# A two-layer perceiver on one core: SP's last stores and loads in another order, two projections and their norms in one block by halves

## The reference, cut to what matters

```python
x = x + xattn0(ctx, layernorm(x), mask)   # 16 heads of 16, masked
x = x + attn0(layernorm(x))               # causal, spectrally scaled weights
x = x + experts(layernorm(x))             # top 3 of 12, two mixtures
x = x + xattn1(layernorm(x), ctx, ctx)    # 16 heads of 64, with a norm of its own
x = x + attn1(layernorm(x))               # covariance scores
x = x + ffn(layernorm(x))                 # quantised, gated
# layernorm(x) = (x - mean) / sqrt(var + 1e-5), over the 256 features
# each attention ends with  out @ Wo ; attn0's Wo is scaled by sigma
```

## Time and profile before

| | us |
|---|---|
| three runs, median (lowest, highest) | 1699.28 (1698.58, 1701.09) |
| the profiled execution, its own time | 1701.46 |
| its span, first to last instruction | 1699.7 |
| PE, DVE, ACT, POOL busy | 1549.9, 1102.9, 890.6, 694.0 |
| mean granted TensorE clock | 0.954 of full |

### The profile page before, as it was taken

How to read it: one execution, slowest core, us unless ns; L and a number is a source line. 1 busy time by engine, 2 the same in 40 slices (tenths; PEclk the granted TensorE clock), 3 DMA queues, 4 the chain that set the end, 5 groups by cost and what they waited for, 6 DMA issues and landing times. The chain is left out here.

```text
span 1699.7 us, 42063 instructions
## 1 busy us (share of the span) xinstructions
PE 1549.9 (91%) x15983; PEld 878.0 (52%) x15983; DVE 1102.9 (65%) x1783; ACT 890.6 (52%) x1205; POOL 694.0 (41%) x539
## 2 busy tenths in 40 slices
PE   7999999999499999999777969999999999996784
PEld 3454554554134343433453426777777777773442
DVE  4656656665499999997327756666666666604546
ACT  5555555554178888888251015555555555541535
POOL 5340000000011111111152209999999999960710
PEclk9999999999689999999898979999999999997897
DMA  7987979877522222221400057555555546212000
GB/s 240 224 239 213 224 232 227 224 213 178 175 79 67 66 67 66 67 67 34 159 2 1 0 143 225 156 159 141 139 156 161 150 121 161 77 36 94 2 1 13
DMA packets 178502, 212.23 MB, mean 125 GB/s; under 512 B 57380, under 2 KB 151856, under 8 KB 173768
## 3 DMA queue, kind: packets, MB, share of 16 engines
q1 hardware_dynamic: 177800, 210.44, 44.9%
q10 hardware_dynamic: 576, 0.00, 0.0%
HBM read 122.78 MB, written 87.57 MB: 124 GB/s over the span
## 5 line engine op out<-in xcount | busy, mean ns | idle before, releaser
L1227 POOL TENSOR_TENSOR x_r<-x_p 128x1024 f16<-128x1024 f32 x256 | 479.3, 1895 | 24.1 <-ACT x_p L1203 17.3
L1242 DVE TENSOR_REDUCE x_mx<-a_all 128x2 f32<-128x1024 f32 x249 | 304.9, 1225 | 147.1 <-PE a_all L1126 147.1
L1203 ACT ACTIVATE x_p<-s_all 128x1024 f32<-128x1024 f32 x256 | 248.4, 1022 | 223.5 <-PE s_all L1109 223.5
L801 ACT ACTIVATE x_p<-s_all 128x1024 f32<-128x1024 f32 x256 | 261.7, 1025 | 60.4 <-PE s_all L708 55.0
L849 DVE TENSOR_REDUCE x_mx<-a_all 128x1 f32<-128x512 f32 x352 | 232.0, 683 | 32.3 <-PE o_all L717 23.2
L1109 PE MATMUL s_all<-x_q,x_k 64*128 64x256 f16 x3072 | 210.2, 270 | 0.0
L1144 PEld LDWEIGHTS o_all<-x_v,x_p 128*128 128x128 bf16 x2048 | 178.7, 97 | 40.1 <-issue 40.1
L1144 PE MATMUL o_all<-x_v,x_p 128*128 128x129 f16 x2048 | 197.3, 221 | 0.9 <-POOL x_r L1227 0.9
L1145 PE MATMUL o_all<-x_v,x_r 128*128 128x65 f16 x2048 | 192.5, 193 | 0.0
L1109 PEld LDWEIGHTS s_all<-x_q,x_k 64*128 64x128 f16 x3072 | 149.5, 94 | 62.2 <-issue 0.8
L1145 PEld LDWEIGHTS o_all<-x_v,x_r 128*128 128x128 f16 x2048 | 180.7, 98 | 0.0
(11 more groups left out here) (367 smaller groups left out, 2759.8 us busy)
## 6 DMA issues: line engine op xcount, KB each, us to landing
values<-vst SPq DMA_DIRECT2D x16, 2064.0 KB, 11.2
x_v<-values SPq DMA_DIRECT2D x32, 1032.0 KB, 5.4
keys<-kst SPq DMA_DIRECT2D x32, 1024.0 KB, 6.9
x_k<-keys SPq DMA_DIRECT2D x128, 256.0 KB, 5.1
wf<-keys SPq DMA_DIRECT2D x192, 64.0 KB, 2.2
values<-vst SPq DMA_DIRECT2D x16, 528.0 KB, 11.6
x_v<-values SPq DMA_DIRECT2D x32, 264.0 KB, 2.6
cf<-in_ctxT SPq DMA_DIRECT2D x16, 512.0 KB, 9.9
```

The costliest lines, as they stand in the source:

```text
L801: act.activation(prob[g % NP][:], chip.s_ps[g % 2][:].rearrange("p (c q) -> p c q", q=SQ), ACT.Exp, scale=hd ** -0.5).then_inc(p_ready, 1)
L1203: act.activation(prob[g % NP][:], chip.s_ps[g % 2][:].rearrange("p (c q) -> p c q", q=SQ), ACT.Exp, scale=hd ** -0.5).then_inc(p_ready, 1)
L1227: pool.tensor_tensor(rest[g % NP][:], prob[g % NP][:], hi, ALU.subtract).then_inc(rest_done, 1)
L1242: dve.tensor_reduce(mx[a[1] % 2][:, n // 4, 2 * (n % 4):2 * (n % 4) + 2], chunk_banks(u, g)[:, :].rearrange("p (h c) -> p h c", h=2), AX.X ...
```

## The change

It has two parts. In SP's program the wait for the query stores and the query loads of w = 0, 1 go behind the last chunk's small stores and the key loads of w = 2, 3; those of w = 2, 3 go into the next block, behind the values of w = 0; the wait for the loads at the end of the block goes. And at two places `project_and_norm` stands for `rows_project` and `layer_norm`: one block, in which transposes, copies, statistics, power, normalising and the second transposes and copies work on two row tiles at a time. ScalarE now copies both halves of the normalised rows.

```diff
--- before
+++ after
@@ project_context, SP's step @@
                             sp.wait_ge(small_stored, 48)
                             for w in range(2, 4):
                                 cross.load_keys(sp, 0, w)
+                            sp.wait_ge(queries.out, 32)
+                            for w in range(2):
+                                cross.load_queries(sp, 0, w)
...
@@ project_context, SP's end @@
                 step(PAIRS - 1, 0, True)
                 queries.stores(sp)
-                sp.wait_ge(queries.out, 32)
-                for w in range(4):
-                    cross.load_queries(sp, 0, w)
                 step(PAIRS - 1, 1, True, final=True)
                 sp.wait_ge(stage_free[0], PAIRS * OUTS * 16 + 16)
                 for w in range(4):
-                    sp.wait_ge(cross.loaded[w], 16 * 12)
                     sp.wait_ge(cross.rows_in[w], 16 * 6)
...
@@ cross_attention_small, SP's start @@
                 sp.dma_start(fold_sb[:], fold).then_inc(fold_in, 16)
-                for w in range(W):
+                buffers.load_values(sp, 0, 0)
+                for w in range(2, W):
+                    buffers.load_queries(sp, 0, w)
+                for w in range(1, W):
                     buffers.load_values(sp, 0, w)
...
+class HalfNorm:
...
+    def stats_of(self, dve, t, src):
+        dve.bn_stats(self.st[:, t, :], src).then_inc(self.stats, 1)
+
+    def variance(self, dve, h):
+        dve.wait_ge(self.stats, 2 * h + 2)
+        for t in (2 * h, 2 * h + 1):
+            dve.bn_aggr(self.mv[:, t, :], self.st[:, t, :]).then_inc(self.spread, 1)
+        dve.wait_ge(self.spread, 2 * h + 2)
+        hs = slice(2 * h, 2 * h + 2)
+        dve.tensor_scalar(self.ve[:, hs], self.mv[:, hs, 1], 1e-5, None, ALU.add).then_inc(self.var, 1)
+
+    def power(self, pool, h):
+        hs = slice(2 * h, 2 * h + 2)
+        pool.wait_ge(self.var, h + 1)
+        pool.tensor_tensor(self.rs[:, hs], self.ve[:, hs], self.chip.half[:, hs], ALU.pow).then_inc(self.rstd, 1)
+
+    def apply(self, dve, t, out, src):
+        dve.wait_ge(self.rstd, t // 2 + 1)
+        dve.tensor_scalar(out, src, self.mv[:, t, 0:1], self.rs[:, t:t + 1], ALU.subtract, ALU.mult).then_inc(self.normed, 1)
+
+    def turn(self, pe, h):
+        pe.wait_ge(self.normed, 2 * h + 2)
+        for k in range(KT):
+            for t in range(2):
+                last = pe.transpose(self.banks[h][:, (2 * k + t) * P:(2 * k + t + 1) * P],
+                                    self.chip.xn[:, 2 * h + t, k * P:(k + 1) * P], self.chip.ident[:])
+        last.then_inc(self.turned, 1)
+
+    def copy(self, act, h):
+        act.wait_ge(self.turned, h + 1)
+        act.activation(self.chip.xnT[:, :, h * 2 * P:(h + 1) * 2 * P], self.banks[h].rearrange("p (k t) -> p k t", k=KT),
+                       ACT.Copy).then_inc(self.copied, 1)
+
+def project_and_norm(chip, tag, src, weight, finish):
...
+            def _(pool):
+                for h in range(2):
+                    norm.power(pool, h)
...
+            def _(pe):
+                for h in range(2):
+                    for k in range(KT):
+                        for t in range(2):
+                            last = pe.transpose(chip.s_banks[h][:, (2 * k + t) * P:(2 * k + t + 1) * P],
+                                                src[:, 2 * h + t, k * P:(k + 1) * P], chip.ident[:])
+                    last.then_inc(tr, 1)
+                pe.wait_ge(weight.loaded, 16)
+                for t in range(NT):
+                    pe.wait_ge(tr_out, t // 2 + 1)
+                    for k in range(KT):
+                        last = pe.matmul(chip.banks[t][:, 0:D], srcT[:, k, t * P:(t + 1) * P], w[:, k, :],
+                                         start=(k == 0), stop=(k == KT - 1))
+                    last.then_inc(ready, 1)
+                for h in range(2):
+                    norm.turn(pe, h)
...
+            def _(act):
+                for h in range(2):
+                    act.wait_ge(tr, h + 1)
+                    act.activation(srcT[:, :, h * 2 * P:(h + 1) * 2 * P], chip.s_banks[h].rearrange("p (k t) -> p k t", k=KT),
+                                   ACT.Copy).then_inc(tr_out, 1)
+                for h in range(2):
+                    norm.copy(act, h)
...
+            def _(dve):
+                for h in range(2):
+                    for t in (2 * h, 2 * h + 1):
+                        dve.wait_ge(ready, t + 1)
+                        finish(dve, t, done)
+                        dve.wait_ge(done, t + 1)
+                        norm.stats_of(dve, t, chip.x[:, t, :])
+                    norm.variance(dve, h)
+                for t in range(NT):
+                    norm.apply(dve, t, chip.xn[:, t, :], chip.x[:, t, :])
...
@@ perceiver @@
-                rows_project(chip, "o0", att, D, wo, add_to_x(chip))
-            layer_norm(chip, "ln1")
+                project_and_norm(chip, "o0", att, wo, add_to_x(chip))
...
-                rows_project(chip, "o1", att, D, wo, finish)
-                layer_norm(chip, "ln2")
+                project_and_norm(chip, "o1", att, wo, finish)
```

More of the change, by code:

```diff
@@ L1271, in _, with __init__ @@
                 output((PAIRS - 1, W - 1))
+class HalfNorm:
+    def __init__(self, chip, tag, scope, banks):
+        self.chip, self.banks = chip, banks
+        self.st = chip.sb(f"{tag}_st", [P, NT, 6], F32, scope)
+        self.mv = chip.sb(f"{tag}_mv", [P, NT, 2], F32, scope)
+        self.ve = chip.sb(f"{tag}_ve", [P, NT], F32, scope)
+        self.rs = chip.sb(f"{tag}_rs", [P, NT], F32, scope)
+        (self.stats, self.spread, self.var, self.rstd, self.normed, self.turned, self.copied) = (
+            chip.sem(f"{tag}_{n}") for n in ("stats", "aggr", "var", "rstd", "xn", "tr", "trout"))
+    def stats_of(self, dve, t, src):
[25 more added lines that the diff above has]
+                       ACT.Copy).then_inc(self.copied, 1)
@@ new lines, in project_and_norm @@
+def project_and_norm(chip, tag, src, weight, finish):
+    nc = chip.nc
+    with ExitStack() as scope:
+        w = weight.w
+        srcT = chip.sb(f"{tag}_srcT", [P, KT, TOK], F32, scope)
+        norm = HalfNorm(chip, f"{tag}_ln", scope, chip.s_banks[2:4])
+        tr, tr_out, ready, done = (chip.sem(f"{tag}_{n}") for n in ("tr", "trout", "rdy", "done"))
+        with nc.Block() as block:
+            @block.gpsimd
+            def _(pool):
+                for h in range(2):
+                    norm.power(pool, h)
+            @block.tensor
+            def _(pe):
[14 more added lines that the diff above has]
+                    norm.turn(pe, h)
+            @block.scalar
+            def _(act):
[5 more added lines that the diff above has]
+                    norm.copy(act, h)
+            @block.vector
+            def _(dve):
[8 more added lines that the diff above has]
+                    norm.apply(dve, t, chip.xn[:, t, :], chip.x[:, t, :])
```

## The result

| us | before | after |
|---|---|---|
| median (lowest to highest) | 1699.83 (1698.58 to 1701.09), 4 runs | 1685.08 (1679.71 to 1686.66), 4 runs |
| the profiled execution | 1701.46 | 1686.49 |
| its span | 1699.7 | 1684.8 |
| mean granted TensorE clock | 0.954 | 0.956 |

The kernel is faster by 14.75 us: ratio 0.9898, with a 95% interval of 0.9881 to 0.9914. The prediction, 1681.6 in a range of 1677.5 to 1687.5, had the sign and the size, and is 3.5 us too low at the median.

The account below looks back on a forecast made before the run. The prediction took SP's program order, and projection, barrier and norm in sequence at two places, as the limits. Gains 8.2 + 8.4 + 1.1 = 17.7 us took the median from 1699.28 to 1681.6, range 1677.5 to 1687.5.

Parts of the forecast that it names:

- SP's order: End of the cross attention's preparation: issuing small stores earlier starts the small attention 8.2 us sooner, bounds 12.2 and 3.2.
- Rival (a): Before the small attention: the small stores land late, SP's reordering gives only 3.2 us, total 1686.6; chance 0.12.
- Rival (e): Before the small attention: another wait near 452 replaces SP's, reordering gains nothing, total 1689.8; chance 0.03.
- The cover for w = 2: In the small attention: w = 2 queries land 5 us before TensorE wants them; beyond that each us late costs one.
- The halved projections: Behind cross attention and self-attention: projection and norm by two tiles gain 8.4 us together, bounds 2.2 and 8.9.
- The clock: At self-attention's start: shorter TensorE idle may hold its clock; a quarter of 4.2 us, 1.1 us, was counted.
- Rival (b): At self-attention's and the experts' start: TensorE's clock holds at both, 3.1 us more gain, total 1678.5; chance 0.17.
- Rival (c): In both norms: GpSimd's powers and VectorE exclude each other, four powers of 0.71 cost 2.8 us, total 1684.4; chance 0.10.

Follow-up runs that it names:

- part 2: The changed kernel with the query loads of w = 2 and 3 moved behind all values and the four weights; one run took 1691.17 us.
- part 3: The changed kernel, but the first pair's normalising waits for both powers, so it runs beside neither; one run took 1688.47 us.
- the kernel with products: Changed kernel, w = 0, 1 queries before small-store wait, causal-mask wait delayed to first scores, six unread products per norm gap; 1679.92 us, again 1681.65.
- Norms alone: Only the two projections with their norms by halves, SP's program as in the kernel before; 1691.78 us, ratio 0.9942.
- part 5: GpSimd's split waits for only the first half of experts' weights: on changed kernel 1684.87 us, with earlier TensorE projections 1681.53, with six idle products too 1677.05.
- part 4: Changed kernel, w = 0, 1 queries before small-store wait, TensorE waiting for the mask only at first scores: 1681.13 us; plus six idle products per norm gap: 1679.92.
- the kernel with the early start alone: Changed kernel, w = 0, 1 queries before small-store wait, TensorE waiting for the causal mask only at first scores; 1681.13 us, ratio 0.9868.

## Why the prediction was right, and where it wasn't

**SP's order: 8.2 forecast, 8.16 in the trace, 8.6 alone in time.** Every step came as worked out: the small stores seen at 431.95 where 431.0 plus the 0.86 that this execution was late are 431.9; 12 query loads 5.51 for 5.5; the block's start 14.15 us behind the first key load (8.74 + 5.5 forecast). Rival (a) fell on the first of these. A stall on issuing, on which (a) rested, did come, but small: the two key and the one value store took 1.40 and 1.17 us, not 0.91 and 0.43, and SP had to wait until 431.95 in any case. That the sum was met to 0.04 is partly luck: with this order the distance to the block's start differs by 2.2 us between profiles (part 2's and part 3's have 44.67 and 45.12, not 43.34). Rival (e) fell with the 8.6 us. The cover for w = 2 was put at 5 us; part 2 issued the loads 5.5 us later (12.4 behind the start instead of 6.9) and lost 2.3, so it was nearer to 3.2, if they also land 5.5 later.

**The halved projections: 8.4 forecast, 5.64 + 3.36 = 9.0 in the trace.** Behind the cross attention a stretch of 10.1 to 10.6 us was forecast and this execution took 9.16: last epsilon, power, normalising and copy stand 6.17, 7.04, 7.81 and 9.16 us behind the first copy, where the sum had 7.5, 8.2, 8.9 and 10.1. The difference is the clock in the projection's own matmuls. The sum took it as it had been, 0.50 from 815.5 to 818.9. Among the twelve profiles with the halved projection the first half's matmuls took 1.96 or 1.97 us in three (this one among them) and 2.71 to 3.48 in nine, and it is no matter of the code: the kernel with products has 1.97 once and 3.02 when it ran again. With them slow the stretch is 9.97 to 10.67 in eight profiles (part 3's, whose edit lengthens it, is the ninth), with them quick 9.16 to 9.37. So the step was sized rightly for the usual case, and this execution had 1.0 us more. Behind self-attention 3.75 at half clock were forecast and 3.36 came (9.80 or 9.81 us in every profile of this kernel's projection with the clock falling in the first transposes of the normalised rows, 9.35 or 9.36 with the products and once without them, where the sum had 9.4 and 9.0): the same four points stand at 6.36, 7.23, 7.99 and 9.81 where the sum had 6.3, 7.1, 7.8 and 9.4. The power was put at 0.71 and beside the normalising took 0.79. A pair's step from the end of its statistics to its power was put at 0.45, where the row that it was taken from gives 0.50 (0.69 less half of 0.38), and it took 0.56. From the end of the last normalising to its copy are 1.22 us, where the sum had 1.05. Norms alone gave 10.4 us of time.

**The clock: 1.1 forecast.** This is the term that failed, in its two inputs and not only in the share taken. "At most half of 8.5, 4.2 us, comes back" added the lower level's price at self-attention and at the experts. The 2.4 us of self-attention were sized rightly (part 5 has 59.25 to 56.83) but could not come back here: GpSimd ends the wait there (part 4), and the trace of before already showed it, with the split over at 865.7 and the first select at 865.65. Only 1.8 to 2.2 at the experts were to be had, and those did not come, since the clock fell at 884.6 once more. Without the products the first product group of self-attention took 3.62 to 3.75 us in all profiles and that of the experts 3.48 to 3.65; with them it was 1.95 or 1.96 and 1.90 in all three. Cutting the idle gap from 5.59 to 2.43 us and putting turns into it was not enough. Rival (b), the clock held at both places, did not occur; when it was brought about, it gave 2.2, not 3.1.

**Rival (c)** would have cost 2.8 us by queueing. Measured are 0.09 per power beside the normalising, and nothing beside the rest. The Trainium skill, "SBUF — State Buffer", section "Who interferes with whom", has the later of two such operations blocked for the whole instruction of the other. The first pair's normalising started at 812.91 and its first tile ended at about 813.28; a power of 0.70 that had waited for that would end at 813.98, and it ended at 813.87. That margin is thin. What the trace does say is the size: 0.09, where queueing behind each other was priced at 0.71. The page speaks of VectorE operations with two inputs from SBUF or in a two-port mode, which casts and `tensor_scalar` can be in, and no run here shows whether the normalising is one. The record does have a hold-up of whole instructions, though not beside a power: at the start of each self-attention VectorE casts the identity beside two memsets of GpSimd. First the kernel after, then the same kernel run again:

```profile
816.29 1.45 DVE L1836 CAST s_ident<-ident 128x128 f16<-128x128 f32 x1 [1.65 <-PEq L1330]
816.72 0.95 POOL L1622 MEMSET s_vf<- 128x1024 f32 x1
...
817.19 0.56 DVE L1836 CAST s_ident<-ident 128x128 f16<-128x128 f32 x1 [1.65 <-PEq L1330]
817.61 1.10 POOL L1622 MEMSET s_vf<- 128x1024 f32 x1
```

In the first the cast ends 0.07 us behind the memset, in the second the memset is the longer by 0.15. The first form stands at 3 of the 28 such places in the fourteen profiles, two of them in this one. So rival (c) was wrong for the power and the normalising, and not for every pair of the two engines.

**Where the 3.5 us are.** The three terms gave 8.16, 9.0 and nothing, and the trace shows 16.08 at the experts. Of what lies between 17.16 and that, 0.86 is the delay ahead of all changes and 0.36 the later return of the clock in the small attention; self-attention's stretch was 0.13 shorter. Another 1.2 were lost behind 1552, in code that nobody touched, and the two traces show on what. At the start of the second self-attention VectorE's cast took 1.45 us beside the memset, in the kernel before 0.57: 0.89 lost. Up to the products with the values 1.85 more were lost, with a granted clock of 0.60 against 0.80 in the first 8 us and of 0.57 against 0.86 in 2 us near the end. The projection behind it gave back 1.69 (its first eight records took 1.97 us, in the kernel before 3.54), the feed-forward's first product lost 1.64 (5.40 for 3.76), and its last ones gave back 1.26. With 0.23 gained between them that is 1.2. So most of it is the clock, which falls at other points of the same code from one execution to the next. It goes with the total as well: of four executions of the kernel after, the mean clocks 0.956, 0.957, 0.958 and 0.962 go with 1686.49, 1686.66, 1683.67 and 1679.71 us. In the second group of runs the same kernel gained 18.5 us against a kernel before that took 1702.21. The forecast's 17.7 lies between the two groups' 14.75 and 18.5. Why the first group gave less is open; its two medians rest on four runs each.

## What to carry to other kernels

Read a queue's program as a timeline of its own: a store whose data are long ready, behind loads whose turn could come later, was worth 8.2 us, and what it displaced was paid for only where a consumer was closer than its cover. Before a gain on one engine is counted, follow the stage to the operation where its results meet another engine's and see how late the other is: here an earlier start and a held clock, 4.2 us on TensorE's side, gave nothing, GpSimd's side gave 0.3 at most, and both together gave 4.4. Cutting a step by halves pays the hand-overs twice, so it is to be summed with the durations of half tiles and a late one named anew at each.

## What the runs showed of the hardware that was not expected

- Six idle products (2.75 us) in each norm's gap kept the granted clock at 1.00 at both places in all three profiles that have them; it had fallen to 0.50 in all eleven without. The stretch around them did not get longer (9.16 us with and without them, with the projection quick).
- Starting the projections 2.1 us sooner did not hold it: in the kernel with the early start alone, the clock was 0.50 from 812.4 to about 819.
- The clock behind the cross attention is not settled by the program: eight records of the projection took from 1.96 to 3.48 us in profiles of the same code.
- A power of two columns takes 0.70 to 0.71 us, of four 1.02 and of one 0.56; beside VectorE's normalising 0.79.
- A cast by VectorE that takes 0.56 or 0.57 us in 25 of 28 places took 1.45 in three, ending 0.07 or 0.08 us behind GpSimd's memset beside it, with the same program; at the second self-attention of the kernel after this cost 0.89 us.
- Four executions of the changed kernel on one chip differ by 7 us of 1685.
